# One subject-mixed matmul a sample: from two samples a DMA in rows of 4096 B to two channels a partition in rows of 8192 B

## The reference

```python
w = weights[subjects]                     # (128, 128, 128), subjects: (128,) of 0..7
out = jnp.einsum('bct,bcd->bdt', x, w)    # x: (128, 128, 1024)
return x + out
```

## Time and profile before

| | |
|---|---|
| median of 3 runs | 335.07 us (334.43 to 335.13) |
| profiled execution: span from its first to its last instruction | 330.9 us |
| profiled execution: its own whole time | not given apart; the median stands for it |
| moved by the DMA engines | 134.78 MB, 407 GB/s over the span |
| packets of the DMA engines | 35893 |
| instructions | 2706 |

### The profile page before, as it was taken

How to read it: one execution, slowest core, us unless ns; L and a number is a source line. 1 busy time by engine, 2 the same in 40 slices (tenths; PEclk the granted TensorE clock), 3 DMA queues, 4 the chain that set the end, 5 groups by cost and what they waited for, 6 DMA issues and landing times.

```text
span 330.9 us, 2706 instructions
## 1 busy us (share of the span) xinstructions
PE 234.2 (71%) x512; PEld 93.6 (28%) x512; DVE 156.8 (47%) x128; POOL 37.8 (11%) x133
## 2 busy tenths in 40 slices
PE   0069999976876866866866866866867767767750
PEld 0024444332332332322322322322322322322310
DVE  0017777745445445445445445445445445445450
POOL 0011111101111111111111111111111111111000
PEclk9999999999999999999999999999999999999995
DMA  7996999999999999999999999999999999999997
GB/s 272 391 409 245 364 420 419 419 421 423 420 420 420 420 421 421 421 422 420 420 420 420 421 422 422 420 420 420 419 421 421 423 421 420 420 420 421 421 421 308
DMA packets 35893, 134.78 MB, mean 407 GB/s; under 512 B 2097, under 2 KB 3122, under 8 KB 35890
## 3 DMA queue, kind: packets, MB, share of 16 engines
q10 hardware_dynamic: 18466, 67.64, 50.3%
q1 hardware_dynamic: 17424, 67.11, 50.0%
HBM read 67.63 MB, written 67.11 MB: 407 GB/s over the span
## 4 chain that ended last, share of the span: by engine, by line
DMA 75%; PE 17%; DVE 3%; issue 1%; ACTq 0%; POOLq 0%; SPq 0%; POOL 0%
DMA out<-ring 46%; DMA ring<-x 24%; PE products L126 17%; DMA table<-weights 5%; DVE ring L142 3%; POOLq L97 0%; ACTq L151 0%; ACTq L168 0%; SPq L82 0%; ACTq L167 0%; POOLq L102 0%; POOLq L92 0%; POOL selected L102 0%
## 5 line engine op out<-in xcount | busy, mean ns | idle before, releaser
L126 PE MATMUL products<-ring,selected 128*128 128x512 f32 x512 | 234.2, 604 | 84.6 <-DMA ring<-x 65.1
L142 DVE TENSOR_TENSOR ring<-products,ring 128x1024 f32<-128x1024 f32 x128 | 156.8, 1225 | 163.2 <-PE products L126 163.2
L126 PEld LDWEIGHTS products<-ring,selected 128*128 128x128 f32 x512 | 93.6, 191 | 224.3 <-issue 162.5
L102 POOL COPY selected<-table 128x128 f32 x128 | 37.6, 294 | 272.7 <-PE products L126 253.0
L185 POOL MEMSET const-float32-0.0<- 128x1 f32 x1 | 0.1, 98 | 0.1
L185 POOL MEMSET const-bfloat16-1.0<- 128x1 bf16 x1 | 0.1, 101 | 0.0
L185 POOL MEMSET const-uint8-127<- 128x1 uint8 x1 | 0.1, 101 | 0.0
L185 POOL MEMSET const-float32-1.0<- 128x1 f32 x1 | 0.1, 98 | 0.0
L185 POOL BASE_LOAD x1 | 0.0, 17 | 0.2 <-issue 0.2
## 6 DMA issues: line engine op xcount, KB each, us to landing
ring<-x SPq DMA_DIRECT2D x63, 1024.0 KB, 11.4
out<-ring ACTq DMA_DIRECT2D x63, 1024.0 KB, 22.9
ring<-x SPq DMA_DIRECT2D x2, 512.0 KB, 10.7
out<-ring ACTq DMA_DIRECT2D x2, 512.0 KB, 10.3
table<-weights ACTq DMA_DIRECT2D x1, 512.0 KB, 16.7
subject_row<-subjects ACTq DMA_DIRECT2D x1, 0.5 KB
```

Source lines behind the costliest of these rows:

```text
L102: nc.gpsimd.tensor_copy(selected[:, k, :], table[:, bass.ds(subject * mixed, mixed)]).then_inc(weights_selected, 1)
L126: product = nc.tensor.matmul(products[:, k, cols], selected[:, k, :], ring[:, s, g, cols], start=True, stop=True)
L142: nc.vector.tensor_tensor(ring[:, s, g, :], products[:, k, :], ring[:, s, g, :], ALU.add).then_inc(sum_ready[k], 1)
```

## The change

A partition now holds two neighbouring channels of a sample, 2q and 2q+1, one behind the other: in memory they are one row of 8192 B. 64 partitions make a sample and 128 make a tile of two samples, which is 1 MB of contiguous memory. The sum over 128 channels becomes two matmuls of 64 rows that add up in PSUM (e = 0, 1); the two samples of a tile (g = 0, 1) lie in the two halves of the array's rows and write to different banks. A tile has eight matmuls where two samples had four.

POOL no longer copies the weights: it adds a matrix `unit` to them that has ones where output channel and input channel are the same, and so the residual x comes out of the matmul. At the same time it reorders the columns, so that output channels 2m go to PSUM partitions 0 to 63 and 2m+1 to 64 to 127. It makes `unit` at the start with a memset and two affine_select. The table stands twice in SBUF, on partitions 0 to 63 and 64 to 127, and is loaded by two DMAs.

VectorE and ACT only copy out of PSUM: VectorE sample 0 of the tile to partitions 0 to 63 of a second ring `out_ring`, ACT sample 1 to partitions 64 to 127, each in two copies of 64 x 1024. PSUM holds two tiles.

All transfers but that of the subjects are issued by SP on one queue: first the table, then eight loads, and from then on, for each tile, the wait for its copies, its store and the load of the tile eight later. The split of the last slot is gone.

The diff, added lines and what stands around them; removed lines are in the kernel above. Semaphores, `ones` and `unit` ([128, 256] each) and asserts are left out.

```diff
+TILES_PER_TURN = 8
+PSUM_BUFS = 2
+SELECT_BUFS = 4
+HALF = 64
 def subject_mix_kernel(nc: bass.Bass, x: bass.AP, subjects: bass.AP, weights: bass.AP, out: bass.AP):
...
+    row = 2 * times
+    tiles = samples // 2
+    turns = tiles // TILES_PER_TURN
     banks = times // BANK
...
+    wide = 2 * mixed
+    x_rows = x.rearrange("b (q e) t -> (b q) (e t)", e=2)
+    out_rows = out.rearrange("b (q e) t -> (b q) (e t)", e=2)
+    w_rows = weights.rearrange("n (q e) d -> q n (e d)", e=2)
...
+        x_ring = ctx.enter_context(nc.sbuf_tensor("x_ring", [channels, TILES_PER_TURN, row], F32))
+        out_ring = ctx.enter_context(nc.sbuf_tensor("out_ring", [channels, TILES_PER_TURN, row], F32))
+        table = ctx.enter_context(nc.sbuf_tensor("table", [channels, n_subjects, wide], F32))
+        selected = ctx.enter_context(nc.sbuf_tensor("selected", [channels, SELECT_BUFS, wide], F32))
...
+        products = ctx.enter_context(nc.psum_tensor("products", [mixed, PSUM_BUFS, 2, times], F32))
...
         @block.sync
         def _(sp):
...
+            for g in range(2):
+                sp.dma_start(table[g * HALF:(g + 1) * HALF], w_rows).then_inc(table_loaded, DMA)
+            for s in range(TILES_PER_TURN):
+                sp.dma_start(x_ring[:, s], x_rows[s * channels:(s + 1) * channels, :]).then_inc(x_loaded[s], DMA)
+            def go_round(turn, last=False):
+                for s in range(TILES_PER_TURN):
+                    tile = turn * TILES_PER_TURN + s
+                    sp.wait_ge(even_drained, 2 * tile + 2)
+                    sp.wait_ge(odd_drained, 2 * tile + 2)
+                    sp.dma_start(out_rows[bass.ds(tile * channels, channels), :],
+                                 out_ring[:, s]).then_inc(stored[s], DMA)
+                    if not last:
+                        sp.dma_start(x_ring[:, s], x_rows[bass.ds((tile + TILES_PER_TURN) * channels, channels), :]
+                                     ).then_inc(x_loaded[s], DMA)
+            with sp.Fori(0, turns - 1) as turn:
                 go_round(turn)
             go_round(turns - 1, last=True)
+            for s in range(TILES_PER_TURN):
+                sp.wait_ge(stored[s], turns * DMA)
         @block.gpsimd
         def _(pool):
+            nc.gpsimd.memset(ones[:], 1.0).then_inc(ones_ready, 1)
+            pool.wait_ge(ones_ready, 1)
+            for g in range(2):
+                part = slice(g * HALF, (g + 1) * HALF)
+                nc.gpsimd.affine_select(unit[part, :], ones[part, :], [[128, 2], [-128, 2], [-1, HALF]],
+                                        ALU.is_equal, 0.0, base=0, channel_multiplier=1).then_inc(unit_ready, 1)
+            pool.wait_ge(unit_ready, 2)
             pool.wait_ge(subjects_loaded, DMA)
...
+            pool.wait_ge(table_loaded, 2 * DMA)
+            def go_round(turn, first=False):
+                for s in range(TILES_PER_TURN):
+                    k = s % SELECT_BUFS
+                    tile = turn * TILES_PER_TURN + s
+                    for g in range(2):
+                        part = slice(g * HALF, (g + 1) * HALF)
+                        subject = pool.value_load(subject_row[0:1, bass.ds(2 * tile + g, 1)],
+                                                  min_val=0, max_val=n_subjects - 1)
+                        if g == 0 and (not first or s >= SELECT_BUFS):
+                            pool.wait_ge(product_ready, tile - SELECT_BUFS + 1)
+                        picked = table[part, bass.ds(subject, 1), :].rearrange(
+                            "p n (e m b) -> p (n e) b m", e=2, b=2)
+                        nc.gpsimd.tensor_tensor(
+                            selected[part, k, :].rearrange("p (e b m) -> p e b m", e=2, b=2), picked,
+                            unit[part, :].rearrange("p (e b m) -> p e b m", e=2, b=2),
+                            ALU.add).then_inc(weights_selected, 1)
             go_round(0, first=True)
             with pool.Fori(1, turns) as turn:
...
         @block.tensor
         def _(pe):
...
+            def go_round(turn, first=False):
+                for s in range(TILES_PER_TURN):
+                    tile = turn * TILES_PER_TURN + s
+                    k, b = s % SELECT_BUFS, s % PSUM_BUFS
+                    pe.wait_ge(x_loaded[s], turn * DMA + DMA)
+                    pe.wait_ge(weights_selected, 2 * tile + 2)
+                    if not first or s >= PSUM_BUFS:
+                        pe.wait_ge(even_drained, 2 * (tile - PSUM_BUFS) + 2)
+                        pe.wait_ge(odd_drained, 2 * (tile - PSUM_BUFS) + 2)
                     for n in range(banks):
...
+                        for e in range(2):
+                            for g in range(2):
+                                part = slice(g * HALF, (g + 1) * HALF)
+                                last = nc.tensor.matmul(
+                                    products[:, b, g, n * BANK:(n + 1) * BANK],
+                                    selected[part, k, e * mixed:(e + 1) * mixed],
+                                    x_ring[part, s, e * times + n * BANK:e * times + (n + 1) * BANK],
+                                    start=(e == 0), stop=(e == 1))
+                    last.then_inc(product_ready, 1)
+            go_round(0, first=True)
+            with pe.Fori(1, turns) as turn:
+                go_round(turn)
         @block.vector
         def _(dve):
             def go_round(turn, first=False):
...
+                for s in range(TILES_PER_TURN):
+                    tile = turn * TILES_PER_TURN + s
+                    dve.wait_ge(product_ready, tile + 1)
+                    if not first:
+                        dve.wait_ge(stored[s], turn * DMA)
+                    for b in range(2):
+                        nc.vector.tensor_copy(out_ring[0:HALF, s, b * times:(b + 1) * times],
+                                              products[b * HALF:(b + 1) * HALF, s % PSUM_BUFS, 0, :]
+                                              ).then_inc(even_drained, 1)
             go_round(0, first=True)
             with dve.Fori(1, turns) as turn:
...
         @block.scalar
         def _(act):
             act.dma_start(subject_row[:], subjects.rearrange("(a b) -> a b", a=1)).then_inc(subjects_loaded, DMA)
...
+            def go_round(turn, first=False):
+                for s in range(TILES_PER_TURN):
+                    tile = turn * TILES_PER_TURN + s
+                    act.wait_ge(product_ready, tile + 1)
+                    if not first:
+                        act.wait_ge(stored[s], turn * DMA)
+                    for b in range(2):
+                        nc.scalar.copy(out_ring[HALF:channels, s, b * times:(b + 1) * times],
+                                       products[b * HALF:(b + 1) * HALF, s % PSUM_BUFS, 1, :]
+                                       ).then_inc(odd_drained, 1)
+            go_round(0, first=True)
+            with act.Fori(1, turns) as turn:
+                go_round(turn)
```

More of the change, by code:

```diff
@@ L24 @@
 I32 = mybir.dt.int32
-GROUP = 2
-SLOTS = 8
-BUFS = 4
+TILES_PER_TURN = 8
+PSUM_BUFS = 2
+SELECT_BUFS = 4
 BANK = 512
 DMA = 16
+HALF = 64
 def subject_mix_kernel(nc: bass.Bass, x: bass.AP, subjects: bass.AP, weights: bass.AP, out: bass.AP):
@@ L71, in _ @@
         def _(sp):
[L72 to L82, removed]
@@ L84, in _ @@
-            go_round(0, first=True)
-            with sp.Fori(1, turns - 1) as turn:
+            for g in range(2):
[12 more added lines that the diff above has]
+                                     ).then_inc(x_loaded[s], DMA)
@@ L91, in _ @@
+            pool.wait_ge(unit_ready, 2)
             pool.wait_ge(subjects_loaded, DMA)
-            pool.wait_ge(table_loaded, DMA)
+            pool.wait_ge(table_loaded, 2 * DMA)
             def go_round(turn, first=False):
[L95 to L103, removed]
+                for s in range(TILES_PER_TURN):
[13 more added lines that the diff above has]
+                            ALU.add).then_inc(weights_selected, 1)
@@ L110, in _ @@
         def _(pe):
[L111 to L123, removed]
-                    for n in range(banks):
[L125 to L128, removed]
+            def go_round(turn, first=False):
[7 more added lines that the diff above has]
+                        pe.wait_ge(odd_drained, 2 * (tile - PSUM_BUFS) + 2)
+                    for n in range(banks):
+                        for e in range(2):
[7 more added lines that the diff above has]
+                    last.then_inc(product_ready, 1)
             go_round(0, first=True)
-            with pe.Fori(1, turns - 1) as turn:
+            with pe.Fori(1, turns) as turn:
                 go_round(turn)
-            go_round(turns - 1, last=True)
         @block.vector
```

46 lines of the change are left out of this document (11 added, 35 removed).

## The result

The changed kernel takes 331.41 us (median of 4 runs, 330.83 to 331.55) against 334.75 us before (4 runs): 0.9907 of it, 95% interval 0.9882 to 0.9932, so 3.1 us or 0.9% faster. 329.0 was forecast, with a gain of 6; by the medians it is 3.3. The profiled execution took 331.55 us over a span of 329.2.

What follows compares the result with a forecast made beforehand. DMA transfers were taken to bound the kernel, 320.1 us of 330.9 at 421 GB/s. Forecast: 2.9 + 3.0 + 316.6 + 2.2 = 324.7 us span, + 4.2 = 328.9, given as 329.0, range 323 to 343.

Steps and rivals of the forecast that it cites:

- start and table: Before x streams: 2.9 us until the DMA engines are full, plus 3.0 us for the table's two copies.
- tail: End of the span: 2.2 us behind the last packets stay, with stores still queued when the last load lands.
- around the span: Time outside the profiled span: 4.2 us, median 335.07 against span 330.9, kept unchanged.
- my upper bound: Table load: 5.2 us, twice the lower bound, if a copy into 64 partitions gets half of the way in.
- The gap: Loss at 24 to 38 us from the late table: 4.6 us, covered by queued loads with some 5 us to spare.
- The rate: Loads and stores in 8192 B rows: mean 424 GB/s, 316.6 us for 134.22 MB; bounds 411 and 433.
- Rival 4: Transfers: rows of 8192 B move no faster, mean 416 GB/s, 334.9 us in all, no change; chance 0.10.
- Rival 1: Transfers: one queue loses rate turning between loads and stores; 338.9 us at 411 GB/s; chance 0.18.
- rivals 2 and 3: TensorE; rival 2: array halves don't run side by side, 6.9 us a tile, about 461 us, chance 0.11.
- rival 3: TensorE: weights not loaded behind a running matmul of the same half, 4.96 us a tile, 358 us; chance 0.05.
- Draining: Copies out of PSUM: VectorE 2.45 us a tile, ACT taken at 1.2 a copy, all beside 4.95 us of transfer.
- the bounds: POOL's two additions a tile: 0.3 to 1.2 us each, 1.4 to 3.2 us a tile, hidden.

Runs made afterwards that it cites:

- e6: Changed kernel with the matmul loops turned, all of sample 0 and then all of sample 1 instead of alternating: 331.05 us, ratio 0.991.
- e7: Kernel before the change with one edit, the table loaded first on SP's queue ahead of x: 328.46 us, ratio 0.9837.
- e3: Changed kernel with the table's second copy (partitions 64 to 127) issued on ACT's queue: 330.77 us, ratio 0.9894.
- e13: Changed kernel with stores on ACT's queue and the table loaded once, ACT copying it to partitions 64 to 127: 327.28 us, ratio 0.9799.
- e17: Changed kernel, still one queue, with the table loaded once and its second half copied by ACT: 328.16 us, ratio 0.9803.
- e2: Changed kernel with both rings padded so that a row of 8192 B goes as two pieces of 4096 B: 334.06 us, ratio 0.9997.
- e5: Changed kernel with stores on ACT's queue and rings padded to give pieces of 4096 B: 333.43 us, ratio 0.9963.
- e9: Changed kernel's transfers alone, without matmuls, copies or choice of weights, storing a constant: 325.62 us, ratio 0.9747.
- e1: Changed kernel with its stores issued by ACT on ACT's queue: 329.85 us, ratio 0.986.
- e14: Changed kernel with only the matmuls of the first of a partition's two channels, 512 recorded MATMULs for 1024: 329.33 us, ratio 0.9836.
- e15: Kernel before with the table first, each matmul over 512 columns cut into two of 256, 1024 recorded MATMULs: 330.07 us, ratio 0.9855.

## Why the prediction was right, and where its terms were not

The direction and the range held, and so did what was to bring the gain, the earlier table and the longer rows; the gain was half of the one forecast, because two costs came out larger. The sum against the profiled execution (the measured tail is what the other terms leave of the span):

| term | forecast | measured |
|---|---|---|
| start and table | 2.9 + 3.0 | 8.1 |
| 134.22 MB | 316.6 (424 GB/s) | 314.3 (427) |
| tail | 2.2 | 6.8 |
| around the span | 4.2 | 2.35 |
| sum | 328.9 | 331.55 |

That the time is only 2.4 us off is in part luck. The span is 4.5 off (324.7 forecast, 329.2 measured): start and tail were 6.8 us too small, and a rate 2.3 too slow and 1.85 too much around the span hid 4.1 of that.

*Start and table* (5.9 forecast, 8.1 measured). By 9 us 1.44 MB had moved, 1.05 of them the table; the other 0.39 are 0.9 us of the middle. The term was mis-sized by 2.2 here, and by 1.3 in e6, the fastest start with the same transfers: the table stood near my upper bound, twice the time a copy. It landed at 9.2 us, where I had 6 to 8. The line drawn through pieces of 512 and 4096 B gave 46 ns for 1024 B; that holds for the first pieces alone, and the mean was 83. The rule of the Trainium skill (SBUF — State Buffer, Door 1: The DMA port swizzle) gave just this 2.2, and the trace agrees: 218 to 223 GB/s while the copies run is about half of 427. The 353 GB/s of e7 rule out the length of the pieces; e3 didn't bring the halves side by side, so no run tests the rule by itself. What avoids the cost is clear: e13 and e17.

*The gap* was covered as foreseen: POOL 10.2, TensorE 11.9, first store 20.95 against a forecast of 19 to 21. e7 shows what it was worth: 5.5 us of 334, and that it needed nothing else of the change. TensorE's first matmuls went at half the pace, as I took it: weight loads are 0.85 us apart until 17.2 us and 0.43 behind that, though the clock column reads 1.00 in both.

*The rate* came out above the forecast, by 2.3 us. In place of a mean of two kinds on a line, one constant does: 4096 B pieces follow each other after 155.5 ns and 8192 B pieces after 306 in the packets of the last engine, so a piece costs 5 ns of its own. Rival 4 is out (e2, e5: 3 to 3.5 us for the long rows). Rival 1 is out: one queue holds 427 GB/s.

*The tail* is the step that failed (2.2 forecast, 6.8 measured). I had the stores queue up behind the last load so that all engines stay busy to the end. Fifteen do. What I took for one stream is sixteen, and one of them fell 4.2 us behind, some 0.7 us a turn, while the engines worked. e9 shows that the engines' work brings the lag; e1, e2 and e5 that queue and rows don't make it. That the number of TensorE's instructions makes it larger isn't shown (e14, e15): it is 3.1 us with 512 MATMULs and 3.0 to 4.9 in the programs with 1024 MATMULs of 64 rows, and e7 ends up to 1.7 us behind where the kernel before, with the same instructions, has 0.5 at most in the last turn. Which engine lags, and by what path the work holds it up, stays open. Whether the recording of the instructions itself does it wasn't tried: every run here was recorded.

*Around the span* I took 4.2 us from a median of 335.07 less a span of 330.9. But the kernel before varies: its runs give time and span together, as 333.3 with 330.9 and 334.25 with 331.8, always 2.4 to 2.5 apart. The profiled execution was a quick one.

*TensorE*: side by side as taken, 3.70 us; rivals 2 and 3 are out. The weight loads of a half lie under running matmuls of the same half too: one pair every 0.43 us with nothing added; so the rule of the Trainium skill that made rival 3 (TensorE: Matmul & The Clock Gate, Part 3: Packing small matmuls) is not borne out here either. *Draining*: VectorE 1.22 us a copy as taken, ACT 1.0. *POOL*: 0.73 us an addition, between the bounds. None of them is ever waited for at the pace of the transfers.

So where the gain went, as an estimate from differences of runs: early table -5.5 (e7), rate -4.5 (318.8 us at 421 GB/s less the 314.3 of the table above; e2 and e5 show 3 to 3.5 of it, their lag being 1 us smaller), second copy of the table +2.0 to +3.5 (e13 against e1, e17 against the changed kernel), lag some +4 (e9). That makes -4.0 to -2.5, and 3.1 to 3.3 were measured.

## What to carry to other kernels

When transfers are the bound, first ask what stands ahead of the first store: moving one 0.5 MB load to the head of the queue was worth more by itself than together with a new layout. Read the last microseconds of a DMA-bound kernel by share: 0.06 is one engine of sixteen, and the mean rate of the middle hides it. Before a difference between two traces is given to an edit, look for it in traces in which the edit can't act yet: the start varied by 0.7 us among seven profiles that begin alike. And take time less span from runs that state both, not from a median and another run's profile.

## What the runs showed of the hardware that was not expected

- With half the matmuls (TensorE busy for 116 of 200 us, 148 in the changed kernel) the granted clock averaged 0.76 from 100 to 300 us (1.00 in the changed kernel), and the transfers still went at 427 GB/s.
- A row of 8192 B moves as one packet of 309 ns, one of 4096 B takes 159.
- Two loads of 64 partitions, issued at the same time on SP's and ACT's queues (e3), ran one behind the other.
- One of the sixteen DMA engines fell behind evenly, by some 0.7 us a turn, while the compute engines worked, and no further once they had stopped.
- Matmuls on two halves of the rows overlap even when the program issues them half by half: 4.1 us a tile, where strict order with one overlap would be 6.4 or more.
- The changed kernel's transfers alone, both copies of the table among them, take 325.6 us (e9); the best version here, e13, is 1.7 us above that, having 0.5 MB less of table to move.
